# A two-layer graph network on one core: one TensorE update for four edge groups, eight exponential buffers, twelve row buffers

## The reference

```
layer 1   m   = relu(x[src]) + 1e-7
          a   = segment_softmax(m over dst)          # per node and per feature
          x1  = layernorm(x + (x + segment_sum(a * m, dst)) @ W0 + b0)
layer 2   Q, K, V = x1 @ Wq + bq, x1 @ Wk + bk, x1 @ Wv + bv      # 8 heads of 12
          E   = edge_attr @ We + be
          s   = exp(clip(sum_head(K[src] * Q[dst] / sqrt(12) * E), -5, 5))
          h   = segment_sum(V[src] * s, dst) / (segment_sum(s, dst) + 1e-6)
          out = layernorm(x1 + h)
```

## Time and profile before

| what | us |
|---|---|
| median of 2 runs (5265.66 to 5273.49) | 5269.57 |
| the profiled execution's own time | 5248.06 |
| span of that execution, first to last instruction | 5246.3 |
| layer one, POOL's gathers | 2.8 to 2537.6 |
| layer two, POOL's gathers | 2594.3 to 5214.7 |
| POOL busy, share of the span | 3240.7, 62% |
| PE busy, share | 3084.1, 59% |

### The profile page before, as it was taken

One profiled execution on the slowest core, in us unless ns is written; L12 is line 12 of the kernel. 1 busy time (PEld: TensorE's weight loads), 2 busy tenths in 40 slices (PEclk: granted clock), 3 DMA queues, 4 the chain that ended last, 5 costly groups with the idle time before them and its releaser, 6 DMA issues.

```text
span 5246.3 us, 52541 instructions
## 1 busy us (share of the span) xinstructions
PE 3084.1 (59%) x16572; PEld 2872.6 (55%) x16572; DVE 1883.1 (36%) x5136; ACT 845.8 (16%) x1933; POOL 3240.7 (62%) x3330
## 2 busy tenths in 40 slices
PE   2445454554454445444566666776667676777776
PEld 2445444444444444444566666665666566666666
DVE  3223222222222222222334444444444444444444
ACT  1212222222222222222201111101101110111111
POOL 6666666666666666666466656666666566666664
PEclk9855555555555555555556666566665656665666
DMA  3111111111111111111133333333333333333333
GB/s 93 37 38 37 42 38 37 36 42 37 37 37 43 37 37 37 43 37 37 46 99 106 103 102 105 104 104 101 106 103 105 99 106 104 103 102 103 106 105 82
DMA packets 277580, 376.85 MB, mean 72 GB/s; under 512 B 140757, under 2 KB 183414, under 8 KB 277302
## 3 DMA queue, kind: packets, MB, share of 16 engines
q0 software_dynamic: 132864, 245.03, 18.2%
q1 hardware_dynamic: 144438, 128.41, 8.5%
HBM read 353.82 MB, written 19.32 MB: 71 GB/s over the span
## 4 chain that ended last, share of the span: by engine, by line
another core or an unknown queue 48%; PE 23%; issue 12%; DVE 9%; ACT 7%; DVEq 0%; ACTq 0%
PE banks L493 6%; PE banks L534 6%; PE banks L523 4%; PE banks L554 3%; ACT ex L633 3%; PE banks L543 3%; ACT relu L626 2%; DVE mt L767 2%; DVE ex L838 1%; DVE prod L902 1%; PE banks L467 1%; DVE score L917 1%; DVE onehot L742 1%; DVE prod L888 1%
## 5 line engine op out<-in xcount | busy, mean ns | idle before, releaser
L405 POOL DMA_INDIRECT rows<-key_value,src_i x1661 | 1625.2, 978 | 1051.8 <-DVE vals L894 517.2
L405 POOL DMA_INDIRECT rows<-in_x,src_i x1661 | 1614.1, 972 | 922.2 <-issue 510.1
L493 PE MATMUL banks<-onehot,ex 128*96 128x64 f32 x6644 | 1074.2, 355 | 1273.6 <-ACT ex L633 713.2
L493 PEld LDWEIGHTS banks<-onehot,ex 128*96 128x96 f32 x6644 | 1039.9, 267 | 1313.6 <-issue 1111.7
L534 PE MATMUL banks<-qw,onehot_t 128*128 128x192 f32 x1664 | 590.5, 503 | 478.4 <-ACT onehot_t L659 378.1
L534 PEld LDWEIGHTS banks<-qw,onehot_t 128*128 128x128 f32 x1664 | 435.1, 299 | 505.2 <-ACT onehot_t L659 399.3
L523 PE MATMUL banks<-we_sb,ea 97*128 97x96 f32 x3322 | 665.5, 366 | 0.3 <-issue 0.3
L523 PEld LDWEIGHTS banks<-we_sb,ea 97*128 97x128 f32 x3322 | 615.6, 276 | 0.0
L848 DVE TENSOR_TENSOR sums<-sums,banks 96x128 f32 x416 | 117.3, 282 | 1343.4 <-remote 1157.7
L554 PEld LDWEIGHTS banks<-onehot,vals 128*104 128x104 f32 x3322 | 575.7, 266 | 1.2 <-DVE vals L894 1.1
L554 PE MATMUL banks<-onehot,vals 128*104 128x64 f32 x3322 | 566.8, 343 | 1.0 <-DVE vals L894 1.0
(11 more groups left out here) (90 smaller groups left out, 1237.9 us busy)
## 6 DMA issues: line engine op xcount, KB each, us to landing
ea<-in_edge_t SPq DMA_DIRECT2D x415, 192.0 KB
rows<-in_x,src_i POOLq DMA_INDIRECT x1661
rows<-key_value,src_i POOLq DMA_INDIRECT x1661
qw<-query SPq DMA_DIRECT2D x832, 24.0 KB
key_value<-qkv SPq DMA_DIRECT2D x24, 384.0 KB
xt<-in_x_t SPq DMA_DIRECT2D x7, 672.0 KB, 11.8
query<-qkv SPq DMA_DIRECT2D x24, 192.0 KB
out<-outs SPq DMA_DIRECT2D x24, 192.0 KB
```

The costliest lines, as they stand in the source:

```text
L405: pool.indirect_dma_start(out=to[0:n, r, u, :], out_offset=None, in_=table, in_offset=bass.IndirectOffsetOnAxis(ap=src_i[0:n, g * G + u:g ...
L493: last = nc.tensor.matmul(ps_sum0[b][:, j, :], ex[:, b, u, j * D:(j + 1) * D], onehot[:, r, u, :], start=u == 0, stop=u == n - 1)
```

## The change

In layer one, PE writes the sums of four groups (a batch) into four parts of one PSUM bank, and only the last matmul of the batch increments `s_sum`. `ex` gets 8 buffers instead of 2 and lies behind `xr` in the memory of `rows`. The one-hot ring has 12 buffers instead of 4. DVE adds four groups at a time, one batch behind. The stages of a chunk stand further behind its last group: on PE after 7, 17 and 18 groups instead of 1, 5 and 6; on ACT after 12, 17 and 18 instead of 2, 5 and 6. `xt` is loaded chunk by chunk into two buffers, and x itself, loaded into `x1`, gives the maximum. In layer two the ring of rows has 12 buffers instead of 6. The diff without the constants that follow from it:

```diff
 R0 = 8
-R1 = 6
-RO = 4
+R1 = 12
+RX = 8
+NB = -(-NG // G)
+RO = 12
...
+def stage_group(c):
+    return last_group(c) if c + 1 < NC else NG + G - 1
...
-        xt = sb("xt", [D, NT * P])
+        xt = sb("xt", [D, 2, CN])
-        ex = sb("ex", [P, 2, G, 2 * D])
+        ex = flat[:, R0 * G * D:(R0 + 2 * RX) * G * D].rearrange("p (a b c) -> p a b c", b=G, c=2 * D)
...
+            def load_nodes(c):
+                n = tiles_of_chunk(c) * P
+                if c >= 2:
+                    sp.wait_ge(s_y, c - 1)
+                sp.dma_start(xt[:, c % 2, 0:n], x_t[:, c * CN:c * CN + n]).then_inc(s_xt[c % 2], 16)
...
             for b in range(XP):
-                sp.dma_start(xt[:, b * XN:(b + 1) * XN], x_t[:, b * XN:(b + 1) * XN]).then_inc(s_x[b], 16)
+                sp.dma_start(x1[:, b * XN:(b + 1) * XN, :], whole[:, b * XN:(b + 1) * XN, :]).then_inc(s_x[b], 16)
+            for c in range(2):
+                load_nodes(c)
...
                 def sum_rows(g):
-                    b, r = g % 2, g % RO
+                    m, r = g // G, g % RO
-                    if g >= 2:
-                        pe.wait_ge(s_add, g - 1)
+                    if g % G == 0 and m >= 2:
+                        pe.wait_ge(s_add, (m - 1) * G)
...
-                    last.then_inc(s_sum, 1)
+                    if g % G == G - 1 or g == NG - 1:
+                        last.then_inc(s_sum, 1)
...
                 def exp_rows(g):
-                    if g >= 2:
-                        act.wait_ge(s_sum, g - 1)
+                    if g >= RX:
+                        act.wait_ge(s_sum, (g - RX) // G + 1)
...
-                        if last_group(c) + 5 == at:
+                        if stage_group(c) + 17 == at:
                             copy_turned(c)
-                        if last_group(c) + 6 == at:
+                        if stage_group(c) + 18 == at:
                             copy_projected(c)
...
                 def add_rows(g, at):
-                    dve.wait_ge(s_sum, g + 1)
+                    dve.wait_ge(s_sum, g // G + 1)
...
                     if g + 2 < NG:
-                        if g >= 2:
-                            dve.wait_ge(s_sum, g - 1)
+                        if g + 2 >= RO:
+                            dve.wait_ge(s_sum, (g + 2 - RO) // G + 1)
                         make_onehot(g + 2, s_oh)
...
+                    if g >= 2 * G - 1 and g % G == G - 1:
+                        first_of = g - 2 * G + 1
+                        cols = group_values(DVE_ENGINE, slot, first_of, RN - 1)
+                        for k in range(G):
+                            add_rows(first_of + k, cols[k])
+                            node_stages(first_of + k)
```

More of the change, by code:

```diff
@@ L41 @@
 XP = 7
-XN = NT * P // XP
+XN = NT // XP
 W1 = D + HEADS
@@ L133, in build @@
         banks = ps("banks", [P, 8, 512])
-        ps_sum0 = [banks[0:D, b, 0:2 * WIN].rearrange("p (a b) -> p a b", b=WIN) for b in range(2)]
+        ps_sum0 = [[banks[0:D, b, 2 * WIN * k:2 * WIN * (k + 1)].rearrange("p (a b) -> p a b", b=WIN)
+                    for k in range(G)] for b in range(2)]
         ps_y = banks[:, 2, 0:CT * D].rearrange("p (a b) -> p a b", b=D)
@@ L147, in build @@
         s_x = [sem(f"s_x{b}") for b in range(XP)]
+        s_xt = [sem(f"s_xt{b}") for b in range(2)]
         s_w = sem("s_w")
@@ L329, in _ @@
                 for c in range(NC):
+                    if c + 2 < NC:
+                        load_nodes(c + 2)
                     store_tables(c)
@@ L438, in _ @@
             pe.wait_ge(s_w, 48)
-            for b in range(XP):
-                pe.wait_ge(s_x[b], 16)
             def nodes_out(c):
                 pe.wait_ge(s_msg, c + 1)
+                pe.wait_ge(s_xt[c % 2], 16 * (c // 2 + 1))
                 if c:
@@ L508, in _ @@
                     node_stages(g - 1)
-                for at in range(NG - 1, NG + 6):
+                for at in range(NG - 1, NG + 24):
                     node_stages(at)
@@ L630, in exp_rows @@
                     act.wait_ge(s_relu, g + 1)
-                    if g >= 2:
-                        act.wait_ge(s_sum, g - 1)
-                    nc.scalar.activation(ex[:, b, 0:n, 0:D], relu[:, b, 0:n, :], ACT.Exp,
+                    if g >= RX:
+                        act.wait_ge(s_sum, (g - RX) // G + 1)
+                    nc.scalar.activation(ex[:, g % RX, 0:n, 0:D], relu[:, b, 0:n, :], ACT.Exp,
                                          bias=gneg[:, :]).then_inc(s_exp, 1)
@@ L651, in _ @@
                     node_stages(g - 2)
-                for at in range(NG - 2, NG + 6):
+                for at in range(NG - 2, NG + 24):
                     node_stages(at)
@@ L746, in _ @@
                 dve.wait_ge(s_x[b], 16)
-                last = V.tensor_reduce(xmax[0:D, b:b + 1], xt[:, b * XN:(b + 1) * XN], AX.X, ALU.max)
+                last = V.tensor_reduce(xmax[:, b:b + 1], x1[:, b * XN:(b + 1) * XN, :], AX.XY, ALU.max)
             link(last)
-            V.tensor_reduce(both[0:D, 0:1], xmax[0:D, :], AX.X, ALU.max).then_inc(s_both, 1)
+            V.tensor_reduce(both[:, 0:1], xmax[:, :], AX.X, ALU.max).then_inc(s_both, 1)
             dve.wait_ge(s_w, 48)
@@ L837, in weigh_rows @@
                     dve.wait_ge(s_exp, g + 1)
-                    V.scalar_tensor_tensor(out=ex[:, b, 0:n, D:2 * D], in0=relu[:, b, 0:n, :], scalar=EPS_MSG,
-                                           in1=ex[:, b, 0:n, 0:D], op0=ALU.add, op1=ALU.mult).then_inc(s_p, 1)
+                    V.scalar_tensor_tensor(out=ex[:, g % RX, 0:n, D:2 * D], in0=relu[:, b, 0:n, :], scalar=EPS_MSG,
+                                           in1=ex[:, g % RX, 0:n, 0:D], op0=ALU.add, op1=ALU.mult).then_inc(s_p, 1)
                 def add_rows(g, at):
-                    dve.wait_ge(s_sum, g + 1)
+                    dve.wait_ge(s_sum, g // G + 1)
                     if g:
@@ L868, in _ @@
                 make_onehot(1, s_oh)
-                for g in range(NG + 1):
-                    if g < NG:
-                        weigh_rows(g)
+                for g in range(NG):
+                    weigh_rows(g)
                     if g + 2 < NG:
-                        if g >= 2:
-                            dve.wait_ge(s_sum, g - 1)
+                        if g + 2 >= RO:
+                            dve.wait_ge(s_sum, (g + 2 - RO) // G + 1)
                         make_onehot(g + 2, s_oh)
-                    if g:
-                        if (g - 1) % 4 == 0:
-                            cols = group_values(DVE_ENGINE, slot, g - 1, RN - 1)
-                        add_rows(g - 1, cols[(g - 1) % 4])
-                        node_stages(g - 1)
-                for at in range(NG, NG + 5):
+                    if g >= 2 * G - 1 and g % G == G - 1:
[4 more added lines that the diff above has]
+                            node_stages(first_of + k)
+                cols = group_values(DVE_ENGINE, slot, NG - G, RN - 1)
+                for k in range(G):
+                    add_rows(NG - G + k, cols[k])
+                    node_stages(NG - G + k)
+                for at in range(NG, NG + 16):
                     node_stages(at)
```

34 lines of the change are left out of this document (18 added, 16 removed).

## The result

The kernel after takes **5459.33 us** (median of 2 runs, 5456.55 and 5462.1) where the one before took 5269.57: **3.6% slower, ratio 1.0358, 95% interval 1.031 to 1.0406**. In a later comparison of the same two it was 5474.38 us (4 runs) against 5268.27 (7 runs), ratio 1.0379 (1.0344 to 1.0414). I had said 5090 us, 3.4% faster. Whatever the edit, the executions lie at one of two levels, which for the kernel before are 5224 to 5294 us ("slow", the level of these results) and 4335 to 4345 us ("quick").

A forecast was written before the change was run, and what follows sets the result against it. POOL's queue was taken as both layers' floor, with waits from PE's late updates on top. Span 5246.3 - 186 (layer one) - 8 (its end) + 15 (layer two) = 5067, plus 23 gives 5090 us; range 4850 to 5225.

The forecast's parts named there:

- What bounds the kernel: Both layers: POOL's queue of gathers is the floor, with some 930 us of POOL's waits on top.
- The reading of the late updates: While POOL issues gathers without pause, PE's semaphore updates come one at a time, some 13 us apart; POOL's pauses release them.
- For the sums alone: Layer one's sums: one update per batch of four, needed every 20.4 us, would remove POOL's waits of 411.5 us.
- Layer one in all, -186: Layer one: POOL stops about once a chunk, 25 chunks of 9 us, leaving 225 of 411.5 us of waits.
- The moved distances: Layer one's chunk stages: standing further back doesn't help the tightest piece, ACT's waits for turned nodes and four projections.
- The end of layer one, -8: POOL's 55.8 us wait for the tables shrinks by 8 us, between 0 and 20, as fewer ring groups remain.
- The start, nothing: Kernel start: the extra xt chunks loaded and DVE reducing 128 rows instead of 96 cost nothing.
- Layer two, +15: Layer two's 12-buffer ring: steady state unchanged, the two ends together add 15 us, between 0 and 30.
- the +30: Layer two's start: POOL fills six more groups of 5.1 us before it pauses, adding 30 us.
- the -15: Layer two's end: POOL is done six groups earlier and the chain runs faster, saving 15 us.
- (d): Rival, ACT's five copies a chunk: updates let out one by one even with POOL quiet; slower, 5472 us; 5%.
- (c): Rival, layer one: pause grows with POOL's run, some 0.2 us per us; little change, 5284 us; 21%.

The follow-up runs named there:

- experiment 2: Kernel after with PE's sums update each group, waits still for whole batches: 5390.78 us beside 5223.86 (slow level), 4339.65 beside 4337.66 (quick).
- experiment 4: Kernel before with 10 records of sums a group for 16, same updates: 5143.61 us beside 5223.86 (slow level); 4343.72 at the quick level.
- experiment 3: Kernel after with an update each group, 2 exponential buffers for 8, ACT's wait for its own group's sums restored: 5248.3 us beside 5223.86 (slow), 4344.06 (quick).
- experiment 5: Kernel before, POOL waiting in layer one after each second group until its rows landed: 5142.93 us beside 5223.86 (slow level), 4607.92 (quick).
- experiment 6: Kernel before, layer one's gathers after the first 8 groups replaced by POOL's direct DMAs of as many rows: 3281.33 and 3279.75 us, both quick level.

## Why the prediction was wrong

- **What bounds the kernel.** Right. POOL's queue was called the floor of both layers, with some 930 us of waits on top (of its sums, 1630 x 1.28 is 2086 and not 2083, which changes nothing). At the quick level the same kernel takes 4337.66 us, 910 less than the 5248.06 of the profiled execution. No trace of it was kept there; in those of its relatives (experiments 2 and 4) POOL waits for next to nobody but at the layers' border.
- **The reading of the late updates. This is the step that failed:** "PE's semaphore updates come through one at a time, some 13 us apart". The 13 us were not the price of an update but, by the experiments, that of the group's 16 records, 0.8 us each. One update of 16 records each 13 us and 16 records each 13 us look the same in a kernel in which every group has one update and at most two groups are under way. The rows of PE misled me: they show a group's 16 records at full pace while it is its completion that is late, and only with more work queued (after) do the starts show it. Experiments 2 (four times the updates, no cost) and 4 (0.62 of the records, 80 us less) part the two. That a record is late inside a run is measured, 0.44 to 2.4 us from start to start; why it is late no run shows.
- **For the sums alone, all 411.5 us of waits gone.** Wrong by that step. The batch's update rides on 64 records, and DVE waits up to 51.2 us for it. I had allowed 20.
- **Layer one in all, -186, the term of the sum that failed.** +179 was measured; in experiment 3 the exponential ring alone was 154. Dropping ACT's wait for the last group but one let POOL run on from 28 to 35 us, into the part of a run in which a record costs 1.5 us or more. Pauses then grew more than in proportion: 10.3 / 35 = 0.29 us for each us of run, where it was 5.5 / 28 = 0.20.
- **The moved distances** did what they were to do at ACT's projection copies (42.9 us in 50 waits in all) and moved the wait to the turn's copy, 398.2 us in 25, up to 31.5.

```profile
ACT x1t L625 <- PE banks L477: 398.2, 25, 31.5
...
ACT qkv L633 <- PE banks L486: 42.9, 50, 2.1
```

- **The end of layer one, -8.** +16.7. I took the backlog to shrink with POOL as the bound; it grew. Even at the quick level the wait is 41.1 us with the change's late stages (experiment 2) and 32.6 and 35.4 without them (experiments 4 and 5).
- **The start, nothing.** Right, the first gather is at 2.82 us before and 2.87 after.
- **Layer two, +15.** Right in the total: +12.8, POOL's waits for the values 503.3 us in 143 for 517.2 in 145, the first run of POOL 70 us, the pause behind it 10.70. The steady state did not change. The same kernel's layer two differs by 7 us between the two traces of before, so how the 12.8 divide into the +30 and the -15 isn't shown.
- **The rivals.** The time lies beside (d), 5472 us, to which I gave 5%, but not by its mechanism: no chain ran on while POOL was quiet, the records came at 0.16 us each once it had stopped. The mechanism is that of (c), a pause that grows with the run, with the slope 0.29 where I had taken 0.2 and ended at "stays where it was". The profile's sign that I had named for it, fewer but much longer pauses, is what came. The rule that I set aside, PE's updates serialising at some 26 ns (the Trainium skill, "TensorE: Matmul & The Clock Gate", section "The cost: per-tile semaphore tail"), would have had the change do nothing. Experiment 2 agrees with it that updates are cheap, though a price of 26 ns is below what its single executions can show; the rule doesn't explain the loss.

No version here that makes the same sums beats the kernel before at both levels. The one with short runs in layer one is 81 us quicker at the slow level and 270 us slower at the quick one. The kernel after itself has no execution at the quick level; with an update each group (experiment 2) it took 4339.65 us there beside 4337.66.

## What to carry to other kernels

When a result is seen late, ask what it rides on, and count that in every way that the kernel allows (updates, records, bytes) before choosing which to save; if they come in fixed proportion, the trace can't tell and an experiment that changes the proportion must come first. A deeper ring in front of the slower engine is a longer leash for the quicker one: where the quick engine's unbroken work slows the others, look at the mean run and the mean pause before and after, not at the number of buffers. And run the old kernel again beside every experiment: here it moved by 18% from one set of executions to another with no edit.

## What the runs showed of the hardware

- PE's matmuls in layer one come late at the slow level in a long unbroken run of POOL's gathers: starts 1.6 us apart on the mean of one group, in steps of some 0.7 us, against 0.16 us a record from some 6 us after POOL's last gather began. Over the whole trace the spacing grows with the length of the run, from 0.13 to 2.4 us. DVE and ACT don't show it: 23 us into a run in the kernel before ACT's exponential ends at 989.06, and DVE's multiplication, which waits for it, starts at 989.10. The Trainium skill, "SBUF — State Buffer", section "Who interferes with whom", counts PE among the engines that wait for no other's accesses. If the cause lies in such accesses, these rows speak against it; no run here shows what the cause is.
- It is there in some sets of executions and not in others, for the same program, and on two chips both were seen. The clock doesn't explain it (experiments 4 and 5), and neither do the DMA queues: the gathers' data ends 2.1 to 2.2 us after a gather's start in either kind, and in an unbroken run POOL's gathers start 1.25 us apart. What differs between the sets stays open.
- The traces of the two levels differ in one more way, and it points to a rival that no run here tests. Each gather tells of its landing by 16 semaphore updates, 26,576 in layer one. At the quick level the traces hold 26,573 of them or more; at the slow level 6005 (before), 4996 (after) and 14,767 (short runs, experiment 5), though all of the updates must have been made, or the kernel would have stopped. So at the slow level the recording of the execution loses most of these events, and fewer of them where POOL's runs are short and PE isn't late. Every execution here has a span and a granted clock, so each was recorded. The recording may itself hold PE's matmuls up, it may only share a bottleneck with them, or the loss may be a mere companion of the level; executions without it would tell, and there are none. Whether the slow level, and with it the loss of 3.6%, exists without the recording is not shown.
- A short idle of POOL clears it: 1.7 us after each 10 us was enough in layer one, where the full ring took 5.5 us after 28.
- A direct DMA took POOL 537 ns where the indirect one with as many rows took 972 (experiment 6 and the kernel before).
